# A graph attention kernel: four sets of edges sorted without padding in place of two padded ones, with lanes broadcast by transfers

## What is computed

```
n_in, n_out = node[recv], node[send]
wn_out = n_out @ W_lin + b_lin
e_ij   = leaky_relu2(concat([n_in, n_out]) @ W_att + b_att)     # slope 0.2
a_ij   = e_ij @ w_alpha
alpha  = exp(a_ij - segment_max(a_ij, recv)) / segment_sum(exp(...), recv)
n_i    = segment_sum(alpha * wn_out, recv)
out    = layernorm(x + elu(n_i))
```

## Time and profile before

| | |
|---|---|
| median of 3 runs | 2518.36 us (2517.06 to 2518.79) |
| profiled execution | 2515.42 us, span 2513.6 us |
| granted TensorE clock, mean | 0.952 |
| TensorE matmuls | 2201.0 us busy, 88% of the span |
| VectorE | 1942.1 us, 77% |
| GpSimd | 1659.3 us, 66% |
| ScalarE | 1293.6 us, 51% |
| first and last gather | 274.3 and 2433.3 us |

### The profile page before, as it was taken

The page is one execution under the profiler, slowest core; times in us unless marked ns, Lnnn a source line. Parts: engine busy times, 40 slices in busy tenths (PEclk is TensorE's granted clock), DMA queues, the critical chain, the costliest instruction groups (busy, mean ns, idle before and its releaser), DMA issues.

```text
span 2513.6 us, 64106 instructions
## 1 busy us (share of the span) xinstructions
PE 2201.0 (88%) x14002; PEld 1568.5 (62%) x14217; DVE 1942.1 (77%) x5224; ACT 1293.6 (51%) x3890; POOL 1659.3 (66%) x1734
## 2 busy tenths in 40 slices
PE   2454599999999999999999999999999999999981
PEld 1232376766676676676677776776666666666651
DVE  9999699987888887888866666676667676766757
ACT  7634376444554455554464444555454444545434
POOL 2000477777777777777777777777777777777750
PEclk8766699999999999999999999999999999999996
DMA  3101233343333333333333333333333333333361
GB/s 94 47 21 34 65 105 105 104 113 102 102 104 105 103 104 105 103 106 103 104 106 107 107 107 107 107 106 105 105 106 106 105 105 106 106 105 105 106 81 51
DMA packets 98809, 243.23 MB, mean 97 GB/s; under 512 B 28514, under 2 KB 41806, under 8 KB 98606
## 3 DMA queue, kind: packets, MB, share of 16 engines
q0 software_dynamic: 82160, 225.44, 33.9%
q1 hardware_dynamic: 16446, 15.31, 2.1%
HBM read 230.79 MB, written 9.84 MB: 96 GB/s over the span
## 4 chain that ended last, share of the span: by engine, by line
PE 65%; DVE 9%; POOL 9%; issue 8%; DMA 5%; ACT 4%; DVEq 0%; POOLq 0%; ACTq 0%
PE hidden_ps L816 20%; PE masked_ps L827 12%; PE turned_ps L846 12%; POOL rows L517 9%; PE turned_ps L838 7%; PE hidden_ps L813 7%; DMA rows<-qv_table,index 5%; PE turned_ps L801 3%; ACT rows L530 2%; DVE keys_a L1110 2%; DVE keys_a L1111 2%; PE masked_ps L826 1%; DVE keys_a L1118 1%; DVE keys_a L1119 1%; PE turned_ps L862 1%
## 5 line engine op out<-in xcount | busy, mean ns | idle before, releaser
L517 POOL DMA_INDIRECT rows<-qv_table,index x1708 | 1639.9, 960 | 689.9 <-issue 484.7
L620 ACT ACTIVATE keys_a<-masked_ps,peaks 128x128 f32<-128x128 f32 x1708 | 487.0, 368 | 692.6 <-DVE peaks L1361 690.6
L816 PE MATMUL hidden_ps<-onehotT,p_part 128*128 128x128 bf16 x5124 | 744.3, 220 | 8.0 <-issue 0.3
L846 PEld LDWEIGHTS turned_ps<-rows,keys_a 128*128 128x128 f32 x3416 | 491.4, 191 | 283.3 <-issue 122.2
L1383 DVE SCALAR_TENSOR_TENSOR sums<-sums,shrink,turned_ps 128x129 f32 x1708 | 587.9, 344 | 85.4 <-issue 24.8
L816 PEld LDWEIGHTS hidden_ps<-onehotT,p_part 128*128 x5124 | 480.2, 96 | 264.2 <-issue 189.1
L846 PE MATMUL turned_ps<-rows,keys_a 128*128 128x129 f32 x3416 | 536.1, 280 | 12.0 <-issue 6.4
L813 PE MATMUL hidden_ps<-identf,rows 128*128 128x128 f32 x1708 | 480.6, 281 | 34.8 <-DMA rows<-qv_table,index 29.7
L827 PE MATMUL masked_ps<-leaky,w_cols 128*128 128x512 f32 x854 | 441.6, 599 | 11.3 <-issue 0.2
L610 ACT ACTIVATE sloped<-hidden_ps 128x512 f32<-128x512 f32 x427 | 255.3, 598 | 324.0 <-PE hidden_ps L816 318.9
L1348 DVE TENSOR_REDUCE lows_a<-masked_ps 128x4 f32<-128x512 f32 x254 | 174.9, 689 | 201.2 <-PE masked_ps L827 200.4
(11 more groups left out here) (203 smaller groups left out, 1425.6 us busy)
## 6 DMA issues: line engine op xcount, KB each, us to landing
rows<-qv_table,index POOLq DMA_INDIRECT x1708
qv_table<-rows SPq DMA_DIRECT2D x24, 257.0 KB, 2.6
out<-x_sb SPq DMA_DIRECT2D x1, 1344.0 KB
out<-x_sb SPq DMA_DIRECT2D x1, 896.0 KB
blocks_a<-unit_blocks POOLq DMA_DIRECT2D x1, 508.0 KB, 5.4
keys_a<-in_src SPq DMA_DIRECT2D x1, 484.0 KB
keys_a<-in_dst SPq DMA_DIRECT2D x1, 484.0 KB
out<-x_sb SPq DMA_DIRECT2D x1, 448.0 KB
```

Source lines behind the costliest of these rows:

```text
L517: g.indirect_dma_start(out=rows[:, j % U, c, :], out_offset=None, in_=table, in_offset=bass.IndirectOffsetOnAxis(ap=index[:, j % U, c:c + ...
L620: last = a.activation(weightsT[:, j % 2, unit], masked_ps[:, j % 2, unit], ACT.Exp, bias=peaks[:, bass.ds(peaks_of(i, j) + 2 + 2 * n, 1)])
L816: mm = t.matmul(whole[:, unit], p_parts[s][:, bass.ds(of[c], F)], onehotT[:, j % 4, unit], start=False, stop=(s == 2), skip_group_check=True)
L846: mm = t.matmul(unit_sums_ps[:, c, :], weights[:, j % 2, c * P:(c + 1) * P], rows[:, j % U, c, F:R], start=True, stop=True)
```

## The change

W becomes 512 and there are four sets. The first three are open: a set of 512 sorted groups ("windows") of 128 keys keeps those whose smallest and largest key are of one block. At most 48 windows are mixed. After the sort the windows are written to DRAM by indirect transfers (`scatter`, on GpSimd) at places such that the 464 kept ones (116 chunks) come first and 48 left ones last; the left ones are loaded as part of the next set, 12 rows of it. Only the last set has pads, 13 rows, and gives 67 chunks. That makes 3 x 116 + 67 = 415 chunks. Counting of blocks and padding are needed for the last set alone, inside the loop. Sets 2 to 4 are sorted inside the loop, two stages per chunk. The comparison that starts a merge reads one side backwards (`compare_mirrored`), so rows need no groups.

A set's lanes are written to DRAM as a list, and SP loads each chunk's 512 lanes from there to all partitions, into one of two buffers; the matmul of `spread_lanes` is gone. Side matmuls have a PSUM bank of their own (`aside`). Running extremes are handed over three times. All chunks are unrolled.

The diff, cut to its core:

```diff
-    W = 1024
+    W = 512
+    OPEN = 3
+    SETS = OPEN + 1
+    WINDOWS = W * P // UNIT
+    LEFT = NB - 1
+    KEPT = WINDOWS - LEFT
+    NO = KEPT // PER
+    NL = -(-((E_L + LEFT * UNIT + PAD_PLACES) // UNIT) // PER)
+    NCHS = [NO] * OPEN + [NL]
+    LANE_RING = 2
...
+            def lanes_of(k):
+                s, n = place(k)
+                if k >= LANE_RING:
+                    sp.wait_ge(onehotT_ready, k - LANE_RING + 1)
+                if n == 0:
+                    sp.wait_ge(lanes_stored[s], 16)
+                sp.dma_start(lanes_all[:, k % LANE_RING, :],
+                             lanes_dram[s][n * CHUNK:(n + 1) * CHUNK].rearrange("(a e) -> a e", a=1).to_broadcast([P, CHUNK])
+                             ).then_inc(lanes_in[k % LANE_RING], 16)
...
+            for k in range(NCH):
+                lanes_of(k)
+                besides(k)
...
+            def scatter(s):
+                pool.wait_ge(aside_out, aside_no["rows", s])
+                pool.wait_ge(placed, s + 1)
+                pool.nop(nofuse=True)
+                for c in range(PER):
+                    g.indirect_dma_start(
+                        out=sorted_dram[s], out_offset=bass.IndirectOffsetOnAxis(ap=place_i[:, c:c + 1], axis=0),
+                        in_=rows_of[:, c * UNIT:(c + 1) * UNIT], in_offset=None,
+                    ).then_inc(scattered, 16)
+
+            scatter(0)
...
-            chunks(pool, gather, U)
+            for k in range(NCH):
+                if k in scatter_at:
+                    scatter(scatter_at[k])
+                gather(k)
...
-            def spread_lanes(i, j):
...
-                t.matmul(spread_ps, identb[:, bass.ds(row, 1)].to_broadcast([P, P]), lane_rows[:, s, c * P:c * P + CHUNK],
-                         start=True, stop=True).then_inc(spread_done, 1)
...
-            def make_onehot(k, j):
-                dve.wait_ge(spread_done, k + 1)
-                if past(k, 4):
+            def make_onehot(k):
+                dve.wait_ge(lanes_in[k % LANE_RING], (k // LANE_RING + 1) * 16)
+                if k >= 4:
                     dve.wait_ge(masked_done, k - 3)
-                v.tensor_scalar(onehotT[:, j % 4, :], spread_ps, part_f[:], None, ALU.is_equal).then_inc(onehotT_ready, 1)
+                v.tensor_scalar(onehotT[:, k % 4, :], lanes_all[:, k % LANE_RING, :], part_f[:], None, ALU.is_equal).then_inc(onehotT_ready, 1)
...
+                for n, (phase, stage) in enumerate(stages):
+                    step_of = compare_mirrored if stage == phase - 1 else compare
+                    step_of(keys[sorting, now, :], keys[sorting, 1 - now, :], 1 << stage).then_inc(compared[s], 1)
+                    done, now = done + 1, 1 - now
+                    if n % 2:
+                        yield
```

More of the change, by code:

```diff
@@ L132, in gnn_kernel @@
+    lanes_dram = [nc.dram_tensor(f"lane_list{s}", [P * W], BF16, kind="Internal").ap() for s in range(SETS)]
     with ExitStack() as ctx:
@@ L355, in gnn_kernel, with blocks_of @@
         assert BATCHES[-1][1] * BY == NB
-        def chunks(eng, step, unrolled):
-            for k in range(unrolled):
-                step(k // U, k % U)
-            with eng.Fori(unrolled // U, LOOPED) as i:
-                for j in range(U):
-                    step(i, j)
-            for k in range(LOOPED * U, NCH):
-                step(k // U, k % U)
-        def blocks_of(engine, i, j, times=1):
+        def blocks_of(engine, k, times=1):
             word = nc.values_load_multi_w_load_instructions(
-                packed[:, bass.ds(i * U + j, 1)],
+                packed[:, k:k + 1],
                 engines=(engine,), min_val=0, max_val=(1 << 30) - 1,
-                skip_runtime_bounds_check_because="they are four counts of blocks of eight bits, each below 64")[1][0]
+                skip_runtime_bounds_check_because="they are four numbers of blocks of eight bits, each below 64")[1][0]
             turn = times.bit_length() - 1
@@ new lines, in _, with stage_index, slope @@
+            rows_out(0)
+            before_out(0)
+            for g in TABLE_LAST:
+                table_pair(g)
+            columns_out(0)
+            def stage_index(k):
+                s, n = place(k)
+                if k >= U:
+                    act.wait_ge(gathered[k % U], k // U * (16 * C))
+                if n == 0:
+                    act.wait_ge(unpacked, s + 1)
+                a.activation(index[:, k % U, :], senders_of[:, s % 2, n, :], ACT.Copy).then_inc(indexed, 1)
+            def slope(k):
@@ new lines, in count_before, with turn_kept @@
+            def count_before(s):
+                pe.wait_ge(windowed, 8 * s + 5)
+                aside_free(("before", s))
+                t.matmul(aside[:, 0:1], earlier[:], mixed_sum[:, PER - 1:PER], start=True, stop=True).then_inc(aside_ps, 1)
+            def turn_kept(s):
+                pe.wait_ge(kept_in[s], 16)
+                aside_free(("cols", s))
+                for c in range(C):
+                    mm = t.transpose(aside[:, c * P:c * P + NO], kept[0:NO, c * P:(c + 1) * P], identf[0:NO, 0:NO])
+                mm.then_inc(aside_ps, 1)
@@ L1218, in second_sort @@
[L1218 to L1230 removed]
+                            last.then_inc(run_done[s], 1)
@@ L1234, in _ @@
+                            assert steps == run_ends[s][run] and now == ends_in[run]
+                        if n % 2 or n == stages - 1:
+                            yield
+            dve.wait_ge(edges_in[0], 32)
+            pack_keys(0, slice(0, P))
+            dve.wait_ge(consts_v, 6)
+            sign_rows(0)
+            dve.wait_ge(prepared[0], 3)
             done, now = 0, 0
             for phase in range(1, LOCAL):
-                if done:
-                    dve.wait_ge(compared[0], done)
@@ L1248, in _ @@
-            half = keys[0][edge_rows, now, :]
-            v.tensor_scalar(half, half, sign_of[edge_rows, 0:1], None, ALU.mult).then_inc(compared[0], 1)
-            done += 1
-            def within(rows, now, done, between=None):
+                    if done:
+                        dve.wait_ge(compared[0], done)
+                    step_of = compare_mirrored if stage == phase - 1 else compare
+                    step_of(keys[:, now, :], keys[:, 1 - now, :], 1 << stage).then_inc(compared[0], 1)
@@ L1260, in within @@
                 for n in range(small + LEAD):
-                    if n == LEAD + 4 and between:
-                        for part in between:
-                            pass
                     for h, stage in ((0, n), (1, n - LEAD)):
```

1472 lines of the change are left out of this document (769 added, 703 removed).

## The result

The changed kernel takes 2350.17 us (median of 4 runs, 2347.53 to 2352.72), the kernel before beside it 2518.1: a ratio of 0.9335, 95% interval 0.9323 to 0.9346. The forecast was 2396 within 2342 to 2465; the time lies 8 us above its lower end. The profiled execution has a span of 2345.8 us at a mean granted clock of 0.955.

The account below looks back on a forecast made before the run. GpSimd's gathers were taken as the bound: 173 + 2074 + 10 + 29 + 25 + 80.3 = 2391 us of span, plus 1.8 and 2.9, gives 2396 us; range 2342 to 2465 us.

Parts of the forecast that it names:

- The bound: Chunk loop: GpSimd's 1660 gathers pace at 1.25 us each, 2074 us from first to last start.
- Rival 1: Chunk loop: TensorE paces, a chunk takes 4.6 us, about 2170 us in total; chance 0.04.
- Scatters: Two scatters inside the loop, 8 indirect transfers on GpSimd's queue, can't hide: +10 us, bounds 0 to 18.
- Sort comparisons: In the loop: 774 comparisons, all 256 wide, hold up gathers: +29 us, bounds 12 and 48.
- The one-hot: Each chunk: now reads bf16 from SBUF and can hold up gathers, 0.06 us x 415 = +25 us, bounds 0 to 125.
- the second moment late in the gather: Within each gather: a possible second sensitive moment, which would double the one-hot's random-phase cost of 0.04 us.
- Rival 2: Chunk loop: the one-hot hits the sensitive moment in every chunk, 83 to 141 us, total 2450 to 2510; chance 0.13.
- TensorE, lanes, hand-overs: In the loop: less TensorE work, lane transfers on SP and three hand-overs between sets each change the time by 0.
- rival 3: Chunk loop: lane transfers pace, slower than before; before's time is reached at 5.35 us a chunk; chance 0.07.
- Rival 4: Before the loop: smaller early gain, first gather at 190 to 200 us, total 2415 to 2425; within the forecast.
- Before the loop: Sort of 154 us, then a chain of 6 and 19 us: first gather at 173 us, bounds 160 and 190.
- The end: From the last gather to the end of the span: 80.3 us as before, with the same code.

Follow-up runs that it names:

- three gathers: Changed kernel with three of its four gathers a chunk, the fourth unit's rows coming by one plain transfer on SP's queue: 2114.97 us.
- the small kernel: Separate kernel, not an edit: 12 stretches of 64 gathers, VectorE beside them with one kind of operation; 0.950 us a gather with nothing beside.

## Why the prediction was right, point by point

*The bound.* GpSimd's gathers, 1.25 us each, 1660 of them: right, 2074 us as forecast. Extra matmuls that cost nothing and three gathers that gave 235 us show it from both sides. Rival 1 is out, though its time for a chunk, 4.6 us, was near the 4.52 that three gathers reached, by luck: the 0.383 us under it was 0.22.

*Scatters.* +10: the eight take 0.96 to 1.00 us and the pause of 0.30, 8 x 1.28 = 10. Right, though from the row of a plain gather.

*Sort comparisons.* +29 forecast; 120 gathers held up by them lost 20.7 us. The mechanism is right, as the table of held gathers and the added comparisons (0.10 us a chunk) show; the size was 8 us too high.

*The one-hot.* +25 forecast, 8.4 measured. The kind was right: it works from SBUF to SBUF like the tensor_scalar of the earlier trace rows, and holds a gather up. What failed is the price of 0.06 us a chunk; it was 0.02. The forecast had it across a moment in 0.24 of 415 cases, 100 times, and 83 gathers were held. But each lost 0.10 us, and nothing points to the second moment late in the gather for which the sum was raised: nearly every late gather fits the one at 0.13 us. Behind the sorts only 10 gathers were held by it, 0.9 us in 115 chunks; that a gather takes 0.948 there is a matter of phase and must not be read as a cost of zero. Rival 2, a hit in every chunk and 83 to 141 us, is out.

*TensorE, lanes, hand-overs.* 112 us of waiting for rows, 92.5% busy in the last stretch, 4.5 us of waiting for lanes: rival 3 never came near. At the hand-overs GpSimd's pause stayed at 0.30 us. Rival 4 wanted a first gather at 190 to 200 us; it came earlier than forecast.

*Before the loop.* 173 forecast, 161.7 measured, inside 160 to 190. The sort was over at 138.5 and not 154. Start and packing took 7 us, not 13. The turns and the table I had at 15 + 10; VectorE waited 7.56 behind the table and 14.7 in all for turned keys. The comparisons were right: 138.5 - 7 - 15 = 116, the sum of my 36, 29, 49 and 2. The chain behind it took 161.7 - 138.5 = 23.2 in place of 19: the scatters' landing 153.5 - 149.3 = 4.1 and the reading back 4.8, where I had set 2.6 for each from transfers on idle queues.

*The end.* 80.3 forecast "with the same code", 67.0 measured. The code is the same, its data are not: the key of the unused places decided whether the last five chunks read one row. I had seen neither the late landings in the trace of before nor the changed constant in the diff as a term.

Sum of the misses: -11 at the start, -17 for the one-hot, -8 for the comparisons, +4 for other operations that held up gathers, -13 at the end, together -45 against 2391: 2346. Nearly all misses point the same way, and the 13 us at the end lay outside every bound of the sum, so the time came within 8 us of the range's lower end. The bound and the sizes of the loop are understood; that the total stayed in the range is in part luck.

## What to carry to other kernels

Ask of each engine whether its pause between operations varies: the one whose pause never does is the bound, even at 70% busy, and its count of operations is the price of everything. Before calling an end or a start "the same code", look at what data it moves: padding that all points to one row costs more per transfer than real data. Don't take a matmul's duration as the room it takes; read the start of the next one. And a mean cost of zero doesn't show that two engines leave each other alone: look at the single instructions that did meet, and count how many of them were late.

## What the runs showed of the hardware

- All 128 descriptors of a gather on one row of 1028 B: packets of 0.769 us in place of 0.160, a DMA share of 0.97 at 77 GB/s, 1.5 us from gather to gather. With the 128 different pad rows there was no such thing.
- A gather is held up by VectorE at one moment, 0.13 us after its start, until the end of an instruction that began at least 0.08 us before it, if that instruction has two SBUF sources in f32 or bf16 or goes from SBUF to SBUF as an f32 copy, an f32 multiplication or a bf16 one-hot (212 of 212 gathers in the small kernel). It isn't by a reduction or by an operation with a PSUM source (0 of 114).
- The bf16 one-hot from SBUF, 0.35 us long, held up 83 gathers of 1660 by 0.10 us each in the changed kernel, and 14 more when 75 were added.
- Two more transfers on SP's queue ahead of it made a scatter of 4 x 128 rows land 3.4 us later.
